# A selective-scan and expert-routing kernel: the router's sigmoid through tanh, shorter VectorE chains, the first norm's turned rows copied by VectorE, and a new order of the work in a batch

## The chip, the cores and the metric

One Trainium2 chip, one of its cores. The metric is the device time of one execution in microseconds (us), of which the median of several runs is taken. Matmuls run on TensorE (PE, with its weight loads as PEld), elementwise work on VectorE (DVE) and ScalarE (ACT), one product of the scan on GpSimd (POOL), and SyncE (SP) issues DMAs.

## The reference

The input x is 32 x 750 x 256 in f32; everything is f32. Three stages follow each other, cut here to what matters:

```python
# 1: per batch row, 3 segments of 256 tokens, every second token kept (128 each)
scores = q @ k.T / sqrt(256)                       # q = k = v = x
h = softmax(scores) @ v
# 2: a selective scan on the layernormed h
x_in, z = split(layernorm(h) @ W_in.T)             # 512 + 512
u = silu(causal_conv4(x_in) + b_conv)
dt = softplus(u @ W_dt.T + b_dt);  Bm, Cm = u @ W_B.T, u @ W_C.T      # 16 states
s_n[t] = exp(dt * A_n) * s_n[t-1] + dt * u * Bm_n;  y = sum_n s_n * Cm_n
h = h + (y * silu(z)) @ W_out.T
# 3: a mixture of 64 experts on the layernormed h
score = sigmoid(layernorm(h) @ gate_w.T);  biased = score + gate_bias
# 8 groups of 8: a group's score is the sum of its two best; 4 groups stay; then the best 8 experts
weight = 2.5 * score[chosen] / sum(score[chosen])
h = h + sum over chosen of weight * expert(layernorm(h))   # at most 256 tokens per expert
```

## The kernel before, in words

The program has three phases. `sequence_phase` does stages 1 and 2 and the routing of stage 3, batch row by batch row (32 of them, called batches here, 384 tokens each). `count_phase` and `expert_phase` do the rest and are not touched.

In `sequence_phase` every engine has a `body` of 16 **steps**, k = 0 to 15, one for each state of the scan. In a step of batch b, ScalarE scales dt\*u by B (`scaled_dbu`, L374, three instructions) and takes the exponentials (`decays`, L386, four) for step k+2; TensorE turns the scaled rows into PSUM `psB` in two pieces (`turn_dbu`, L926, 4 and 8 transposes); VectorE scans in two pieces (`scan_piece`, L615, 512 and 1024 wide); GpSimd multiplies by C (L356); and TensorE sums over the states three steps later (`sum_y`, L938). `psB` has one copy: the first piece of step k+1 is turned only once the first piece of step k has been scanned, the second only after the second.

Around these steps each engine carries work of other batches, at places written out by hand in the four `body` functions: the attention of batch a = b+2, the projections, convolution and dt of n = b+1, the gate and output of m = b-1, the second norm of o = b-2, and the routing of c = b-3 (before, the router's logits themselves belong to o). Each engine runs its list in order and waits by semaphore. Small products pass through two PSUM buffers, `psM`: `SLOTTED` lists by name which product uses which buffer in which order (XN: turned rows of the first norm; X: input projection; Z: gate; D: dt; CB, BT: B and C; DU: dt\*u; YT, O: gated y and output; QT, S, PT, AT: attention; X2T: turned rows of the second norm; LG: router logits), and `LAG` which batch it belongs to. A product waits until the one before it in its buffer has been copied out. The steady batches run in a hardware loop of two batches per pass; six batches before and five after are written out.

What the change and the steps of the prediction touch:

- ScalarE's `copy_turned` (L396) copies XN, QT and X2T out of PSUM. XN0 and XN1 are copied in step 0.
- `biased_dt` (L422, L423) and `softplus` (L430, L432): an Identity and an Abs per chunk, then an Exp and a Ln per half.
- `exp_logits` (L481) is the exponential for the router's sigmoid, in step 15; on VectorE `score_experts` (L736, L738) adds one and takes the reciprocal. `score_groups` (L756 to L769) finds the two best of each group by maxima and minima, in nine instructions.
- `silu_z` (L411), `silu_u` (L416) in steps 3 and 4, with the activation table loaded before (at L411) and after (L542).
- VectorE's `row_max` (L632, L635), `newton` (L651 to L658, four instructions on three columns, twice per batch), `conv` (L712, three taps for two pairs of chunks), `gate` (L627), `norm` (L667), `add_block` (L694).
- TensorE's `turn_normed1`, `turn_normed2`, `turn_x` (all L947), `project_xin` (L995), `project_z` (L1003), `project_dt` (L1013), `project_out` (L1052), `route` (L1062).

## Time and profile before

| | |
|---|---|
| three runs | 3473.83, 3476.50, 3476.91 us; median 3476.5 |
| profiled execution | 3474.01 us; span of its instructions 3472.2 us |
| mean granted TensorE clock | 0.955 of full speed; 1.00 from 100 to 2300 us |
| busy, share of the span | PE 86%, PEld 69%, DVE 83%, ACT 82%, POOL 61% |
| HBM traffic | 68 GB/s over the span |

Busy time is the time in which an engine executes an instruction; starts and ends of one instruction overlap with its neighbours' a little. The batches run until about 2980 us, the experts from there on. A wait is put down to the instruction that released it; "issue" is idle time for which the profile shows no releaser.

### The profile page before, as it was taken

The numbers are of one execution on the slowest core, as the hardware profiler recorded it, in microseconds if no ns is written. First come the engines' busy times: TensorE is split into PE (matmuls) and PEld (weight loads), VectorE is DVE, ScalarE is ACT, GpSimd is POOL, SyncE is SP. The second block draws the span as 40 slices with busy tenths as digits, with TensorE's granted clock in tenths as the row PEclk, the third lists the DMA queues.
The fourth block names the chain that finished last, engine by engine and source line by source line (L and its number), as shares of the span: only waits on it lengthen the run. The fifth ranks groups of instructions, "written<-read, shape, count | busy, mean of one in ns | idle before, by whom it ended". The sixth has DMA issues, their size and how long they took to land. (4 is left out here: it accounts for less than half of the span.)

```text
span 3472.2 us, 62460 instructions
## 1 busy us (share of the span) xinstructions
PE 2993.6 (86%) x19009; PEld 2407.9 (69%) x19009; DVE 2874.4 (83%) x4756; ACT 2853.9 (82%) x5580; POOL 2104.8 (61%) x780
## 2 busy tenths in 40 slices
PE   6899999999999999999999999999999997576664
PEld 4777777777777777777777777777777776455543
DVE  3888999999989999999999999999999998444432
ACT  5999999999999999999999999999999995211110
POOL 0666665666656565656565666666666665177776
PEclk8999999999999999999999999999999998578887
DMA  2111222111212121112221211111211110267774
GB/s 92 51 51 60 62 62 63 50 57 62 62 63 62 54 62 48 54 61 62 63 62 63 62 59 57 63 62 63 62 63 62 58 53 27 89 142 150 149 150 81
DMA packets 187542, 241.44 MB, mean 70 GB/s; under 512 B 45152, under 2 KB 165440, under 8 KB 187200
## 3 DMA queue, kind: packets, MB, share of 16 engines
q1 hardware_dynamic: 162624, 199.44, 18.5%
q0 software_dynamic: 24576, 37.77, 6.5%
q8 instruction: 174, 2.85, 0.3%
q14 instruction: 168, 1.38, 0.1%
HBM read 176.07 MB, written 61.08 MB: 68 GB/s over the span
## 5 line engine op out<-in xcount | busy, mean ns | idle before, releaser
L356 POOL TENSOR_TENSOR hid<-hid,c_all 128x1536 f32<-128x1536 f32 x512 | 1770.2, 3457 | 1160.9 <-DVEq L610 1159.4
L615 DVE TENSOR_TENSOR_SCAN hid<-decay,hid,psB 128x1024 f32<-128x1024 f32 x512 | 1201.6, 2347 | 101.8 <-PE psB L926 60.4
L386 ACT ACTIVATE decay<-dt,a_neg 128x383 f32<-128x383 f32 x2048 | 1086.7, 607 | 0.0
L374 ACT ACTIVATE dbu_t<-dtu_t,b_t 128x512 f32<-128x512 f32 x1536 | 994.6, 715 | 41.6 <-PE psB L926 38.1
L926 PE MATMUL psB<-ident,dbu_t 128*128 128x128 f32 x6144 | 856.9, 276 | 109.8 <-DVE hid L615 103.8
L926 PEld LDWEIGHTS psB<-ident,dbu_t 128*128 128x128 f32 x6144 | 701.5, 141 | 234.6 <-DVE hid L615 133.3
L938 PE MATMUL psY<-ident,hid 128*128 128x128 f32 x6144 | 765.3, 275 | 4.0 <-DVE yz_t L627 3.6
L938 PEld LDWEIGHTS psY<-ident,hid 128*128 128x128 f32 x6144 | 695.3, 142 | 6.9 <-issue 3.8
L615 DVE TENSOR_TENSOR_SCAN hid<-decay,psB 128x512 f32<-128x512 f32 x512 | 623.8, 1218 | 72.4 <-PE psB L926 29.7
L1013 PE MATMUL psM<-u,w_dt 128*128 128x384 f32 x1024 | 355.0, 490 | 21.2 <-ACT turned L396 16.8
L1013 PEld LDWEIGHTS psM<-u,w_dt 128*128 128x128 f32 x1024 | 184.4, 190 | 131.4 <-ACT turned L396 23.7
L1427 ACT ACTIVATE e_side<-e_psL,e_in_tile 128x128 f32<-128x128 f32 x128 | 45.7, 363 | 260.0 <-DVE e_in_tile L1551 174.1
L1400 POOL DMA_INDIRECT out_dram<-e_ys,e_dst_st x128 | 205.1, 1602 | 72.5 <-issue 62.1
L712 DVE SCALAR_TENSOR_TENSOR u<-xin,w_cv,u 128x384 f32<-128x384 f32 x384 | 210.8, 611 | 12.5 <-ACT xin L404 12.3
L1003 PE MATMUL psM<-w_in,turned 128*128 128x512 f32 x384 | 178.4, 601 | 36.3 <-ACT zs_t L411 36.3
L995 PE MATMUL psM<-turned,w_in 128*128 128x384 f32 x512 | 182.2, 497 | 4.8 <-ACT xin L404 2.5
L1052 PE MATMUL psM<-w_out,yz 128*128 128x256 f32 x768 | 179.0, 383 | 0.8 <-ACT yz L468 0.8
L1513 DVE COPY e_xt<-e_psG 128x512 f32<-128x512 f32 x64 | 44.2, 691 | 156.4 <-PE e_psG L1453 137.9
L1453 PE MATMUL e_psG<-e_ident,e_xg 128*128 128x128 f32 x256 | 50.6, 330 | 131.6 <-DMA e_xg<-x_weights_dram,e_src_st 131.6
L1391 POOL DMA_INDIRECT e_xg<-x_weights_dram,e_src_st x128 | 127.5, 996 | 49.2 <-issue 37.8
L1052 PEld LDWEIGHTS psM<-w_out,yz 128*128 128x128 f32 x768 | 142.7, 193 | 18.4 <-issue 1.1
L396 ACT ACTIVATE turned<-psM 128x384 f32<-128x384 f32 x192 | 92.2, 481 | 75.2 <-PE psM L947 74.4
(149 smaller groups left out, 3348.3 us busy)
## 6 DMA issues: line engine op xcount, KB each, us to landing
c_all<-bc_rows_dram SPq DMA_DIRECT2D x128, 768.0 KB, 4.8
out_dram<-h SPq DMA_DIRECT2D x64, 384.0 KB, 5.6
h<-out_dram SPq DMA_DIRECT2D x32, 384.0 KB, 4.0
x_weights_dram<-normed SPq DMA_DIRECT2D x32, 384.0 KB, 3.3
xs<-in_x_dram SPq DMA_DIRECT2D x32, 256.0 KB
e_wg<-in_gate_dram SPq DMA_DIRECT2D x64, 128.0 KB
e_wu<-in_up_dram SPq DMA_DIRECT2D x64, 128.0 KB
e_wd<-in_down_dram SPq DMA_DIRECT2D x64, 128.0 KB
```

The costliest lines, as they stand in the source:

```text
L356: nc.gpsimd.tensor_tensor(hid[k % 4][:, :, :], hid[k % 4][:, :, :], c_all[:, k, :].unsqueeze(1).to_broadcast([P, CH, L]), ALU.mult).then_i ...
L374: last = nc.scalar.activation(dbu_t[k % 2][:, t, :], dtu_t[q][:, t, :], ACT.Copy, scale=b_t[q][:, t, k:k + 1])
L386: last = nc.scalar.activation(decay[k % 4][:, c, 1:L], dt[q][:, c, 1:L], ACT.Exp, scale=a_neg[:, c, k:k + 1])
L615: nc.vector.tensor_tensor_scan(h[:, lo:hi], flat(decay[k % 4])[:, lo:hi], flat(psB)[:, lo:hi], h[:, lo - 1:lo] if j else 0.0, ALU.mult, AL ...
L712: last = nc.vector.scalar_tensor_tensor(out=u[:, c, :], in0=xin[:, c, t:t + L], scalar=w_cv[:, c, t:t + 1], in1=u[:, c, :], op0=ALU.mult, ...
L926: last = nc.tensor.transpose(flat(psB)[:, i * P:(i + 1) * P], dbu_t[k % 2][:, t, c * P:(c + 1) * P], ident[:, :])
L938: last = nc.tensor.matmul(psY[:, t, c * P:(c + 1) * P], hid[k % 4][:, c, t * P:(t + 1) * P], ident[:, :], is_transpose=True, start=(k == 0 ...
L995: last = nc.tensor.matmul(psM[slot(name)][:, 0:L], w_in[:, k, c * P:(c + 1) * P], turned[:, k, :], start=(k == 0), stop=(k == KD - 1))
L1003: last = nc.tensor.matmul(psM[slot(name)][:, :], turned[:, k, t * P:(t + 1) * P], w_in[:, k, DI:2 * DI], start=(k == 0), stop=(k == KD - 1))
L1013: last = nc.tensor.matmul(psM[slot(name)][:, 0:L], w_dt[:, k, c * P:(c + 1) * P], u[:, k, :], start=(k == 0), stop=(k == CH - 1))
L1052: last = nc.tensor.matmul(psM[slot(name)][:, i * D:(i + 1) * D], yz[:, c, s * P:(s + 1) * P], w_out[:, c, :], start=(c == 0), stop=(c == C ...
L1400: nc.gpsimd.indirect_dma_start(out=h_out, out_offset=bass.IndirectOffsetOnAxis(ap=dst_st[q][:, h:h + 1], axis=0), in_=ys[q % 4][:, h, :], ...
```

## The change

The router's sigmoid is computed as 0.5 + 0.5 tanh(x/2): ScalarE takes the tanh in step 4, just before the third silu of the gate, one batch later than the exponential was taken (LG's lag goes from -2 to -3), and VectorE needs one instruction instead of two. TensorE's `route` moves from step 15 to step 4. The two best of a group are found in seven instructions. A Newton step has three instructions instead of four. The row maximum is taken negated in one instruction, its scale being put into the turned q (= k), D^-0.25 in QT0 and QT1. Abs of softplus reads SBUF, once per half, instead of PSUM once per chunk. XN0 and XN1 are turned at the end of the batch before (step 15) and copied out of PSUM by VectorE in step 0. Most side work gets new places in the 16 steps, and `SLOTTED` follows them. `DIAG` is empty, so the branches on it add nothing.

```diff
-ROUTE_STEPS = 15
+ROUTE_STEPS = 14
...
-SLOTTED = (("XN0", "X0", "X2", "Z0", "Z2", "D0", "D1", "D2", "X2T0", "D3", "AT0", "BT", "YT0", "DU1", "DU2",
-            "LG"),
-           ("O1", "XN1", "X1", "X3", "Z1", "QT0", "QT1", "S", "PT", "CB", "X2T1", "AT1", "YT1", "DU0", "YT2",
-            "O0"))
...
+SLOTTED = (("X0", "X2", "Z0", "Z2", "D0", "D1", "D2", "X2T0", "D3", "CB", "AT0", "YT0", "DU1", "O0", "XN1"),
+           ("O1", "X1", "X3", "Z1", "LG", "QT0", "QT1", "S", "PT", "X2T1", "BT", "AT1", "YT1", "DU0", "YT2",
+            "DU2", "XN0"))
+LAG = {**dict.fromkeys(("QT0", "QT1", "S", "PT", "AT0", "AT1", "XN0", "XN1",), 2),
+       **dict.fromkeys(("X0", "X1", "X2", "X3", "Z0", "Z1", "Z2", "D0", "D1", "D2", "D3", "CB", "BT", "DU0", "DU1", "DU2",), 1),
...
+       **dict.fromkeys(("O1", "X2T0", "X2T1",), -2),
+       **dict.fromkeys(("LG",), -3)}
...
+                by = D ** -0.25 if name in ("QT0", "QT1") else 1.0
+                nc.scalar.activation(to[:, kd, :], psM[slot(name)][:, 0:L], ACT.Copy,
+                                     scale=by).then_inc(s_out[slot(name)], 1)
...
-                nc.scalar.activation(xin[:, c, TAPS - 1:], src, ACT.Identity, bias=b_dt[:, c:c + 1])
-                nc.scalar.activation(soft[:, c, :], src, ACT.Abs, bias=b_dt[:, c:c + 1]).then_inc(s_out[slot(name)], 1)
+                nc.scalar.activation(xin[:, c, TAPS - 1:], src, ACT.Identity,
+                                     bias=b_dt[:, c:c + 1]).then_inc(s_out[slot(name)], 1)
...
+                nc.scalar.activation(soft[:, a:z, :], xin[:, a:z, TAPS - 1:], ACT.Abs).then_inc(s_de[half], 1)
+                act.wait_ge(s_de[half], 2 * n + 1)
...
+                                                bias=nmax[:, s:s + 1],
...
                 nc.scalar.activation(denom[:, :, :], psM[slot("LG")][:, 0:NSEG * NE].rearrange(
-                    "p (s e) -> p s e", s=NSEG), ACT.Exp, scale=-1.0).then_inc(s_out[slot("LG")], 1)
+                    "p (s e) -> p s e", s=NSEG), ACT.Tanh, scale=0.5).then_inc(s_out[slot("LG")], 1)
...
                     if k == 0:
                         if front:
-                            copy_turned("XN0", n, 0)
-                            copy_turned("XN1", n, 1)
+                            copy_xin(n, 0)
...
                     if k == 4:
+                        if routed:
+                            tanh_logits(c)
                         if front:
                             silu_z(n, r, 2)
                             silu_u(n)
                             act.preload_act_table_set("natural_log_exp_and_others")
-                        if early:
-                            copy_turned("QT0", a, 0)
...
+                        if early:
+                            probs(a)
...
                     if k == 9:
+                        if late:
+                            copy_turned("X2T1", o, 1)
...
-                    if k == 15:
-                        if late:
-                            exp_logits(o)
...
+            def copy_turned(name, b, kd):
+                filled(name, b)
+                to = turned2 if name in ("X2T0", "X2T1") else turned
+                nc.vector.tensor_copy(to[:, kd, :], psM[slot(name)][:, 0:L]).then_inc(s_out[slot(name)], 1)
...
-                nc.vector.tensor_reduce(rmax[:, :], psM[slot("S")][:, 0:L].rearrange("p (s k) -> p s k", s=NSEG),
-                                        AX.X, ALU.max).then_inc(s_rm, 1)
-                dve.wait_ge(s_rm, a + 1)
-                nc.vector.tensor_scalar(nmax[:, :], rmax[:, :], -(D ** -0.5), None, ALU.mult).then_inc(s_nm, 1)
+                nc.vector.tensor_reduce(nmax[:, :], psM[slot("S")][:, 0:L].rearrange("p (s k) -> p s k", s=NSEG),
+                                        AX.X, ALU.max, negate=True).then_inc(s_nm, 1)
...
-                dve.wait_ge(s_nw[j], 3 * n + 1)
-                nc.vector.tensor_tensor(t[:, 1, :], t[:, 0, :], y, ALU.mult).then_inc(s_nw[j], 1)
-                dve.wait_ge(s_nw[j], 3 * n + 2)
-                nc.vector.tensor_scalar(t[:, 2, :], t[:, 1, :], -0.5, 1.5, ALU.mult, ALU.add).then_inc(s_nw[j], 1)
-                dve.wait_ge(s_nw[j], 3 * n + 3)
-                nc.vector.tensor_tensor(rstd[j][:, :], t[:, 2, :], y, ALU.mult).then_inc(s_rs[j], 1)
+                dve.wait_ge(s_nw[j], 2 * n + 1)
+                nc.vector.scalar_tensor_tensor(out=t[:, 1, :], in0=t[:, 0, :], scalar=-0.5, in1=y,
+                                               op0=ALU.mult, op1=ALU.mult).then_inc(s_nw[j], 1)
+                dve.wait_ge(s_nw[j], 2 * n + 2)
+                nc.vector.scalar_tensor_tensor(out=rstd[j][:, :], in0=t[:, 1, :], scalar=1.5, in1=y,
+                                               op0=ALU.add, op1=ALU.mult).then_inc(s_rs[j], 1)
...
-                nc.vector.tensor_scalar(flat(denom), flat(denom), 1.0, None, ALU.add).then_inc(s_rt, 1)
+                after(dve, s_wgt, m)
+                nc.vector.tensor_scalar(flat(score), flat(denom), 0.5, 0.5, ALU.mult, ALU.add).then_inc(s_rt, 1)
+
+            def pair_experts(m):
+
                 routed_to(m, 1)
-                nc.vector.reciprocal(flat(score), flat(denom)).then_inc(s_rt, 1)
-
-            def pair_experts(m):
-
-                routed_to(m, 2)
                 nc.vector.tensor_tensor(biased[:, :, :], score[:, :, :],
                                         bias[:, :].unsqueeze(1).to_broadcast([P, NSEG, NE]), ALU.add).then_inc(s_rt, 1)
+                routed_to(m, 2)
+                grp = biased[:, :, :].rearrange("p t (g h k) -> p (t g) h k", g=G, h=2)
+                nc.vector.tensor_tensor(halves[:, 0, :, :], grp[:, :, 0, :], grp[:, :, 1, :], ALU.max)
+                nc.vector.tensor_tensor(halves[:, 1, :, :], grp[:, :, 0, :], grp[:, :, 1, :], ALU.min).then_inc(s_rt, 1)
+
+            def score_groups(m):
+
                 routed_to(m, 3)
-                grp = biased[:, :, :].rearrange("p t (g h k) -> p (t g) h k", g=G, h=2)
-                hi, lo = halves[:, 0, :, :], halves[:, 1, :, :]
-                nc.vector.tensor_tensor(hi, grp[:, :, 0, :], grp[:, :, 1, :], ALU.max)
-                nc.vector.tensor_tensor(lo, grp[:, :, 0, :], grp[:, :, 1, :], ALU.min).then_inc(s_rt, 1)
-
-            def score_groups(m):
-
-                hi, lo = halves[:, 0, :, :], halves[:, 1, :, :]
-                hi2, mn, mx, lo2 = (quarters[:, j, :, :] for j in range(4))
+                nc.vector.tensor_tensor(quarters[:, 0:2, :, :], halves[:, :, :, 0:2], halves[:, :, :, 2:4], ALU.max)
+                nc.vector.tensor_tensor(quarters[:, 2, :, :], halves[:, 0, :, 0:2], halves[:, 0, :, 2:4],
+                                        ALU.min).then_inc(s_rt, 1)
                 routed_to(m, 4)
-                nc.vector.tensor_tensor(hi2, hi[:, :, 0:2], hi[:, :, 2:4], ALU.max)
-                nc.vector.tensor_tensor(mn, hi[:, :, 0:2], hi[:, :, 2:4], ALU.min)
-                nc.vector.tensor_tensor(mx, lo[:, :, 0:2], lo[:, :, 2:4], ALU.max).then_inc(s_rt, 1)
+                nc.vector.tensor_tensor(quarters[:, 1, :, :], quarters[:, 1, :, :], quarters[:, 2, :, :],
+                                        ALU.max).then_inc(s_rt, 1)
                 routed_to(m, 5)
-                nc.vector.tensor_tensor(lo2, mn, mx, ALU.max).then_inc(s_rt, 1)
-                v = [best[:, j, :] for j in range(4)]
-                nc.vector.tensor_tensor(v[0], hi2[:, :, 0], hi2[:, :, 1], ALU.max)
-                nc.vector.tensor_tensor(v[1], hi2[:, :, 0], hi2[:, :, 1], ALU.min)
+                nc.vector.tensor_tensor(best[:, 0:2, :], quarters[:, 0:2, :, 0], quarters[:, 0:2, :, 1], ALU.max)
+                nc.vector.tensor_tensor(best[:, 2, :], quarters[:, 0, :, 0], quarters[:, 0, :, 1],
+                                        ALU.min).then_inc(s_rt, 1)
                 routed_to(m, 6)
-                nc.vector.tensor_tensor(v[2], lo2[:, :, 0], lo2[:, :, 1], ALU.max).then_inc(s_rt, 1)
+                nc.vector.tensor_tensor(best[:, 1, :], best[:, 1, :], best[:, 2, :], ALU.max).then_inc(s_rt, 1)
                 routed_to(m, 7)
-                nc.vector.tensor_tensor(v[3], v[1], v[2], ALU.max).then_inc(s_rt, 1)
+                nc.vector.tensor_tensor(flat(gsum), best[:, 0, :], best[:, 1, :], ALU.add).then_inc(s_rt, 1)
+
+            def pick_groups(m):
...
+                    if k == 0:
+                        if front:
+                            copy_turned("XN0", n, 0)
+                            copy_turned("XN1", n, 1)
                     if k == 1:
                         if late:
                             add_block(o, 1)
                             second_stats(o)
-                    if k == 3:
+                    if k == 2:
                         if back:
                             gate(m, r)
+                    if k == 4:
                         if front:
                             conv(n, 0, 1)
+                            conv(n, 1, 1)
+                            conv(n, 0, 2)
+                            conv(n, 1, 2)
+                            conv(n, 1, 3)
+                            conv(n, 0, 3)
+                    if k == 5:
                         if late:
                             newton(o, 1)
-                        if front:
-                            conv(n, 0, 2)
-                            conv(n, 1, 1)
-                    if k == 4:
-                        if front:
-                            conv(n, 1, 2)
-                            conv(n, 0, 3)
-                            conv(n, 1, 3)
+                            norm(o, 1, h2, normed2)
                     if k == 6:
                         if routed:
                             score_experts(c)
-                        if late:
-                            norm(o, 1, h2, normed2)
+                    if k == 7:
                         if routed:
                             pair_experts(c)
-                    if k == 7:
-                        if routed:
                             score_groups(c)
+                            pick_groups(c)
+                            pick_experts(c)
                     if k == 8:
-                        if routed:
-                            pick_groups(c)
                         if early:
                             row_max(a)
+                        if routed:
+                            choose(c)
                     if k == 9:
-                        if routed:
-                            pick_experts(c)
                         if front:
                             finish_dt(n, r, 0)
                         if routed:
-                            choose(c)
+                            weigh(c)
                     if k == 10:
                         if front:
+                            drive(n, r, 0)
                             finish_dt(n, r, 1)
-                        if routed:
-                            weigh(c)
-                        if front:
-                            drive(n, r, 0)
+                            drive(n, r, 1)
                     if k == 11:
                         if early:
                             attended(a)
-                        if front:
-                            drive(n, r, 1)
                     if k == 12:
                         if early:
                             first_stats(a)
-                    if k == 14:
+                    if k == 15:
                         if early:
                             newton(a, 0)
-                    if k == 15:
-                        if early:
                             norm(a, 0, h1, normed1)
                         if back:
                             add_block(m, 0)
@@ -915,16 +920,22 @@
...
                     if k == 0:
-                        if front:
-                            turn_normed1(n, 0)
                         if late:
                             project_out(o, 1)
                         if front:
-                            turn_normed1(n, 1)
+                            project_xin(n, 0)
                     if k == 1:
                         if front:
-                            project_xin(n, 0)
+                            project_xin(n, 1)
                     if k == 2:
                         if front:
-                            project_xin(n, 1)
                             project_xin(n, 2)
                             project_xin(n, 3)
...
                             project_z(n, 2)
+                        if routed:
+                            route(c)
+                    if k == 5:
                         if early:
                             turn_x(a, 0)
-                    if k == 5:
                         if front:
                             project_dt(n, 0)
                     if k == 6:
@@ -1113,11 +1123,11 @@
                     if k == 7:
                         if front:
                             project_dt(n, 2)
+                        if late:
+                            turn_normed2(o, 0)
                         if early:
                             scores(a)
                     if k == 8:
-                        if late:
-                            turn_normed2(o, 0)
                         if front:
...
-                    if k == 10:
                         if late:
                             turn_normed2(o, 1)
+                    if k == 10:
+                        if front:
+                            turn_b(n)
                         if early:
                             attend(a, 0)
...
-                            turn_dtu(n, 1)
                     if k == 13:
-                        if front:
-                            turn_dtu(n, 2)
                         if back:
                             turn_yz(m, 2)
+                        if front:
+                            turn_dtu(n, 1)
                     if k == 14:
+                        if front:
+                            turn_dtu(n, 2)
                         if back:
                             project_out(m, 0)
                     if k == 15:
-                        if late:
-                            route(o)
+                        if early:
+                            turn_normed1(a, 0)
+                            turn_normed1(a, 1)
```

## Rows read from the trace of the kernel before

**Rows 1.** Windows: start:end, length, then busy us and (instructions) per engine, clock, DMA.

```profile
700.00:2300.00 1600.00, 1469.94 (x9772) 1184.85 (x9771) 1483.09 (x2242) 1532.87 (x2902) 973.70 (x283) 1.00 0.19 60
...
2985.00:3472.20 487.20, 308.52 (x1270) 242.20 (x1269) 186.43 (x709) 76.98 (x329) 333.46 (x260) 0.78 0.65 130
```

**Rows 2.** Waits from 700 to 2300 us: us in total, times, longest.

```profile
DVE hid L615 <- PE psB L926: 40.8, 76, 2.4
...
ACT turned L396 <- PE psM L947: 32.8, 35, 1.0
...
ACT dbu_t L374 <- PE psB L926: 23.1, 9, 3.5
...
DVE hid L615 <- ACT decay L386: 6.9, 12, 1.8
...
ACT yz L468 <- PE psM L947: 5.4, 17, 0.4
```

**Rows 3.** Groups by line from 700 to 2300 us: busy and mean ns, then idle before.

```profile
L411 ACT ACT_TABLE_LOAD x18 | 23.1, 1283 | 0.3
```

**Rows 4.** Timeline of ScalarE, steps 0 to 4 of one batch: start, us.

```profile
1414.73 0.47 ACT L396 ACTIVATE turned<-psM 128x384 f32<-128x384 f32 x1
1416.02 0.49 ACT L396 ACTIVATE turned<-psM 128x384 f32<-128x384 f32 x1 [0.82 <-PE psM L947]
1416.40 2.12 ACT L386 ACTIVATE decay<-dt,a_neg 128x383 f32<-128x383 f32 x4
...
1434.49 1.28 ACT L411 ACT_TABLE_LOAD   x1
1435.79 1.09 ACT L411 ACTIVATE zs_t<-psM 128x512 f32<-128x512 f32 x2
...
1438.60 0.60 ACT L411 ACTIVATE zs_t<-psM 128x512 f32<-128x512 f32 x1
1439.07 1.49 ACT L416 ACTIVATE u<-u 128x1536 f32<-128x1536 f32 x1
...
1595.34 0.47 ACT L396 ACTIVATE turned<-psM 128x384 f32<-128x384 f32 x1
```

**Rows 5.** Timeline of VectorE: what becomes of the logits, and the scaled row maximum.

```profile
1444.37 0.23 DVE L736 TENSOR_SCALAR denom<-denom 128x192 f32<-128x192 f32 x1
...
1445.90 0.96 DVE L667 TENSOR_SCALAR normed<-h,mv,rstd 128x256 f32<-128x256 f32 x3
...
1458.21 0.17 DVE L635 TENSOR_SCALAR nmax<-rmax 128x3 f32<-128x3 f32 x1
```

**Rows 6.** Groups of VectorE reading PSUM, by shape.

```profile
L1513 DVE COPY e_xt<-e_psG 128x512 f32<-128x512 f32 x64 | 44.2, 691 | 156.4 <-PE e_psG L1453 137.9 <-issue 18.4
...
L694 DVE TENSOR_TENSOR h<-psM,h 128x256 f32<-128x256 f32 x32 | 12.8, 400 | 4.3 <-PE psM L1052 4.3
```

**Rows 7.** Timeline of ScalarE, softplus.

```profile
1456.53 0.58 ACT L423 ACTIVATE soft<-psM,b_dt 128x384 f32<-128x384 f32 x1
1456.99 0.86 ACT L430 ACTIVATE soft<-soft 128x768 f32<-128x768 f32 x1
1457.88 0.85 ACT L432 ACTIVATE soft<-soft 128x768 f32<-128x768 f32 x1
```

**Rows 8.** Timeline of all engines around the loop's back edge.

```profile
1501.26 0.65 PE L926 MATMUL psB<-ident,dbu_t 128*128 128x128 f32 x4 [2.35 <-issue]
...
1502.11 1.22 DVE L615 TENSOR_TENSOR_SCAN hid<-decay,psB 128x512 f32<-128x512 f32 x1 [1.99 <-PE psB L926]
...
1504.13 2.35 DVE L615 TENSOR_TENSOR_SCAN hid<-decay,hid,psB 128x1024 f32<-128x1024 f32 x1 [0.81 <-PE psB L926]
```

**Rows 9.** Timelines of TensorE (routing logits, third gate product) and VectorE (last taps).

```profile
1408.60 1.45 PE L1062 MATMUL psM<-w_gt,turned 128*128 128x64 f32 x12
...
1436.44 1.98 PE L1003 MATMUL psM<-w_in,turned 128*128 128x512 f32 x4 [1.18 <-ACT zs_t L411]
...
1434.02 3.24 DVE L712 SCALAR_TENSOR_TENSOR u<-xin,w_cv,u 128x384 f32<-128x384 f32 x6
```

102 lines of the change are left out of this document (50 added, 52 removed).

## The prediction

> **What bounds the kernel now.** First the windows: the batches fill the time to about 2980 us, and the experts take the last 487.2 us at their own pace, with GpSimd and DMA the busiest; nothing in them is edited [rows 1]. So what the change is worth is read from the steady batches. The same copy of XN0 stands at 1414.73 and, two batches on, at 1595.34 us: 180.6 us for a pass of the loop, **90.3 us per batch** [rows 4]. The 1600 us from 700 to 2300 hold 283 instructions of GpSimd, one per step, or 283 / 16 = 17.7 batches [rows 1]. Divided by that, TensorE is busy 83.0 us per batch, VectorE 83.8, ScalarE 86.6 [rows 1]: three engines near the limit, and no single one that bounds.
>
> Then the waits [rows 2]. VectorE's scans wait 40.8 us for turned rows and 6.9 for decays, 2.7 us per batch; the rest of its idle time is gaps between its own dependent instructions. So 90.3 - 2.7 = 87.6 us of a batch are VectorE's own. ScalarE waits 32.8 + 23.1 + 5.4 us, 3.5 per batch; 86.8 are its own. A change that takes work from only one of the two gains little; this one takes from both.
>
> One wait has a cause apart from the work. At the loop's back edge TensorE stands still for 2.35 us before the first transposes of step 0, with no releaser, and VectorE then loses 1.99 + 0.81 = 2.8 us [rows 8], once in two batches, so 1.4 of its 2.7 us per batch. ScalarE's wait for the same transposes is the 23.1 us in 9 times of [rows 2].
>
> **The change part by part, per batch.** VectorE first.
> - Logits: from the add (1444.37) to the norm behind the reciprocal (1445.90) are 1.53 us; one scalar instruction of 0.23 us stays [rows 5]: -1.3.
> - Two instructions fewer in finding the two best of a group, one fewer in each of two Newton steps, one fewer in the row maximum. The removed ones are small, like the scaled row maximum's 0.17 us [rows 5]. The last three give -0.5; the first two -0.2, since one of the remaining is wider (between 0 and -0.34).
> - The copies of XN0 and XN1 come to it. No row shows 384 columns from PSUM to SBUF alone; 256 wide an add takes 0.40 us and 512 wide a copy 0.69 [rows 6]. Halfway is 0.55, so +1.1 for both, between 0.8 and 1.4.
>
> Sum -0.9 (-1.3 to -0.5). But the copies stand in step 0, ahead of the scan that waits at the back edge. In every second batch they fall into that 2.8 us wait, if the turned rows are there: TensorE now turns them before the back edge. That hides half of their cost: -0.55 more.
>
> ScalarE: from the first copy (1414.73) to the decays behind the second (1416.40) are 1.67 us, of which 0.82 is a wait for TensorE [rows 4]; so -0.85 of work and a wait gone. Abs: one of 384 columns from PSUM takes 0.46 us from its start to the next, four of them 1.8; the Exp of 768 columns takes 0.89 to the start of the Ln that depends on it, and two Abs of that form cost 1.8 [rows 7]. So -0.05 and no more: the gain is only that TensorE gets the D slots back 0.46 us earlier. The tanh costs what the exponential did, and the scale in the q copies is an immediate: 0. Sum -0.9: 85.9 us its own.
>
> For such a copy the Trainium skill speaks against moving it ("VectorE: DVE Perf Modes", the TRN2 errata): it gives 120 + N cycles from PSUM on VectorE and 172 + N on ScalarE. At its clocks (0.96 and 1.2 GHz) that is an estimated 0.53 and 0.46 us for 384 columns; this trace agrees on ScalarE with 0.47 [rows 4]. By it the two copies would cost 1.05 us where the sum has 1.1, so dearer than on the engine they leave, which only matters where VectorE bounds.
>
> TensorE: the same matmuls; 83.0 us stay, and it is the engine with room.
>
> **The moved work.** Step 4 gets worse for ScalarE. Before, the third gate product started at 1436.44 behind a wait of 1.18 us for the first silu and took 1.98 [rows 9]; the third silu began at 1438.60 [rows 4], just in time. Now TensorE adds the routing logits, 1.45 us [rows 9], and ScalarE wants them **ahead** of the third silu. That is a new wait of some 1.3 us; behind it queue the silu of u, the table load, the decays of step 6 and TensorE's first dt product. Against it go the 0.82 us of XN1, and the rest of the 32.8 us that copies of turned rows wait (32.8 / 17.7 - 0.8 = 1.0), mostly X2T0, which is now turned a step earlier. So ScalarE's waits go from 3.5 to 3.5 - 0.8 - 1.0 + 1.3 = 3.0, and its chain to 85.9 + 3.0 = 88.9.
>
> The convolution becomes one block of six passes in step 4; three passes took 3.24 us [rows 9], so 6.4 together. No work is added, and the gate moves from step 3 to 2, where it may wait for the last `sum_y`; and in step 15 the first output product comes one dt\*u turn later and scan piece 1 with it. I put these at +0.15 on VectorE, nothing at best and 1.0 at worst. VectorE: 90.3 - 0.9 - 0.55 + 0.15 = 89.0, which meets ScalarE's 88.9. The router's SP stores, the C loads and GpSimd move by less than a step and are covered by GpSimd's 39% of idle time (973.70 busy of 1600 [rows 1]); without that cover each step would cost GpSimd's own 3.5 us, still under VectorE's.
>
> **Forecast:** 90.3 - 89.0 = 1.3 us per batch, 32 batches, 42 us. Before the first and behind the last scan the chains get some tenths shorter and a table load for the tanh may come: nothing. The profiled execution took 3474.0 us, 0.07% under the median of 3476.5. 3474 - 42 = **3432 us**, with its own range from 0.7 to 1.9 us per batch: 3413 to 3452.
>
> **Rivals.**
> - **More waits go than work.** The new places even out TensorE's list: of the four input projections one falls in step 0, one in step 1 and two in step 2, where there were none, one and three. If VectorE's 1.3 us of waits away from the back edge go too and step 4 costs nothing, 1.45 + 1.05 = 2.5 us per batch: 3394. ScalarE allows it (85.9 plus half of the back edge is about 87). For: both engines lose work. Against: the step 4 wait. 23%.
> - **Given back.** The new waits of steps 2, 4 and 15 take 1.0 us more than assumed: within 0.2% of before, about 3474. 10%.
> - **Slower: ScalarE held twice at step 4.** First by the routing logits, then by the silu of u, which needs the end of the convolution block. Before, ScalarE had 1.9 us in hand there: the last passes began at 1434.02 and took 3.24, the silu began at 1439.07 [rows 4, 9]. Its other waits after the change are 1.7 us, so it is even with before at 90.3 - 85.9 - 1.7 = 2.7 us in step 4, and decides from there. If scans 2 and 3 run late and the block ends 2.4 us behind ScalarE's arrival, on top of 1.3, that is 3.7: 1.0 us per batch slower, 3474 + 32 = 3506. For: six passes in a row with nothing for TensorE to turn. Against: the passes' inputs are ready long before, and the gate and Newton no longer stand between them. 11%.
> - **The tanh is not in the silu's table.** Then each batch has a load before and after it, 1.28 us each [rows 4], 2.6 on ScalarE: 85.9 + 2.6 + 2.7 of waits = 91.2, +0.9 per batch, 3503. No row of this trace shows a tanh; against it: one load serves the three silus of a batch and the Copies that ScalarE scales rows with between them (18 loads in 17.7 batches [rows 3]), so the silu's table holds more than the silu. 3%. 
>
> **Chances.** Forecast 53%, 3394 23%, equal 10%, slower 11% + 3%. A measurement here tells about 0.2% (7 us) from no change. Faster by more than that 0.76, within it 0.10, slower 0.14. The range, 3388 to 3472, holds the forecast and most of the better case, and leaves out the equal and slower ones.
>
> **What the profile after would show.** Right: a spacing of batches near 89.0 us; the reciprocal gone; VectorE's new copies about 0.55 us each, without wait behind the back edge; ScalarE's wait on turned rows below 1 us per batch, and one of about 1 us at the tanh for the logits; two table loads per batch as before; VectorE's wait at the back edge around 1.5 us. Wrong: a wait at the tanh or silu of u over 2.7 us; more than two loads; copies at 0.7 us or more; gate or scan pieces of steps 2, 3 and 15 that wait over 1 us; or a spacing under 88.4, by which waits would have gone and not only work.

## The result, and the profile after

The changed kernel takes 3447.8 us (median of 4 runs, 3442.8 to 3450.8): a ratio of 0.9917 to before, 95% interval 0.9900 to 0.9934. A second measurement, among the experiments, gives 0.9936 [0.9922, 0.9949]; one of its six runs took 7641 us; it is left out of the ratio, and nothing on record explains it. Forecast were 3432 us with a range of 3388 to 3472. The direction and the range are right, the gain is smaller: 29 us, or by the second measurement 22, where 42 were forecast. In this document 1% of 3472 us over 32 batches is 1.085 us per batch, so the gain is **0.7 to 0.9 us per batch** instead of 1.3. The experiments ran on two chips, each beside the kernel before on the same chip; where a run is compared with after across them, both of after's ratios are taken as bounds.

The window over the steady batches answers to [rows 1], with 286 steps of GpSimd, 17.9 batches, where 283 stood:

```profile
700.00:2300.00 1600.00, 1476.54 (x9901) 1193.73 (x9900) 1493.68 (x2182) 1532.84 (x2860) 988.80 (x286) 1.00 0.19 60
```

Divided by 17.9, VectorE is busy 83.5 us per batch (before 83.8): the work that was taken from it hardly shows. ScalarE's fell from 86.6 to 85.7.

ScalarE's timeline gives the period by the copy of X0, two batches apart, and step 4 (start, duration, idle time before in brackets):

```profile
1408.75 0.67 ACT L415 ACTIVATE u<-psM,b_cv,w_cv 128x384 f32<-128x384 f32 x1 [0.34 <-PE psM L1006]
...
1431.94 0.33 ACT L496 ACTIVATE denom<-psM 128x192 f32<-128x192 f32 x1 [1.04 <-PE psM L1073]
1432.17 0.59 ACT L424 ACTIVATE zs_t<-psM 128x512 f32<-128x512 f32 x1
1432.64 1.49 ACT L429 ACTIVATE u<-u 128x1536 f32<-128x1536 f32 x1
...
1587.87 0.67 ACT L415 ACTIVATE u<-psM,b_cv,w_cv 128x384 f32<-128x384 f32 x1 [0.34 <-PE psM L1006]
```

179.12 us for two batches, 89.56 per batch, where [rows 4] had 90.3. Both are passes in which TensorE ran at full clock throughout. That was not so in all: taken from one silu of u to that two batches on, ten passes from about 630 to 2430 us, TensorE's granted clock fell for a stretch to the lower of its two levels (1.2 instead of 2.4 GHz) in 4 of 10 passes of before, in 1 of after and in 4 of the second measurement of after. The passes without such a stretch took 180.3, 179.1 and 179.1 us on average, those with it 1.4 to 2.2 more. At full clock the change is thus worth 0.6 us per batch. The 1.00 that the table of before has from 100 to 2300 us is a rounded mean over these stretches.

The tanh waits 1.04 us for the logits; the silu of u behind it waits for nothing.

The waits from 700 to 2300 us (total, times, longest), against [rows 2]:

```profile
ACT dtu_t L476 <- PE psM L958: 22.0, 18, 1.2
...
ACT denom L496 <- PE psM L1073: 18.7, 18, 1.0
DVE hid L626 <- PE psB L937: 16.1, 28, 0.8
...
PE psM L958 <- ACT xin L435: 12.9, 18, 0.8
ACT u L415 <- PE psM L1006: 12.4, 17, 1.1
...
ACT dbu_t L385 <- PE psB L937: 9.6, 18, 1.2
...
DVE turned L635 <- issue: 7.0, 9, 1.0
...
DVE yz_t L643 <- ACT xin L417: 5.4, 9, 0.8
```

VectorE's waits for others fell from 2.7 us per batch to (16.1 + 5.4) / 17.9 = 1.2. So waits went, 1.5 us, and VectorE's own list, 89.56 - 1.2 = 88.4 (0.4 of it the idle time without a releaser at the back edge), did not get shorter than the 87.6 of before. ScalarE waits 62.7 / 17.9 = 3.5 us as before, at new places; its own work is 89.56 - 3.5 = 86.1 (before 86.8). One wait is to be remembered, that of TensorE's turning (L958) for the copy `xin` (L435): 0.7 us in each batch, for which the trace of before shows no wait.

The groups by line show VectorE's copies and the table loads ahead of the first silu; behind the silu of u there are as many, 18 (busy, mean ns, idle before):

```profile
L424 ACT ACT_TABLE_LOAD x18 | 23.1, 1283 | 0.3
...
L635 DVE COPY turned<-psM 128x384 f32<-128x384 f32 x35 | 17.7, 547 | 7.0 <-issue 7.0
```

Around the back edge, TensorE's and VectorE's timeline, where [rows 8] had 2.35, 1.99 and 0.81:

```profile
1491.00 2.35 DVE L626 TENSOR_TENSOR_SCAN hid<-decay,hid,psB 128x1024 f32<-128x1024 f32 x1 [0.79 <-PE psB L937]
1493.42 0.65 PE L937 MATMUL psB<-ident,dbu_t 128*128 128x128 f32 x4 [1.80 <-DVE hid L626]
1494.19 1.02 DVE L635 COPY turned<-psM 128x384 f32<-128x384 f32 x2 [0.84 <-issue]
```

VectorE loses 0.84 us there and 0.79 in the scan ahead of it, not 2.8. Over the nine back edges from 700 to 2300 us the first of the two is 0.66 to 1.00 us. Before, the two waits together took 2.1 to 2.8 us at full clock, so that the 2.8 of [rows 8] is the largest, and 3.8 to 3.9 where the clock had fallen.

Where did VectorE's removed work go? Its timeline in steps 6 and 7:

```profile
1439.08 0.23 DVE L751 TENSOR_SCALAR score<-denom 128x192 f32<-128x192 f32 x1
1439.23 1.22 DVE L626 TENSOR_TENSOR_SCAN hid<-decay,psB 128x512 f32<-128x512 f32 x1
...
1442.90 0.33 DVE L756 TENSOR_TENSOR biased<-score,bias 128x192 f32<-128x192 f32 x1
...
1445.28 0.31 DVE L786 MAX8 gtop<-gsum 128x8 f32<-128x8 f32 x3 [0.15 <-DVE gsum L779]
...
1447.62 1.22 DVE L626 TENSOR_TENSOR_SCAN hid<-decay,psB 128x512 f32<-128x512 f32 x1
```

The logits cost 0.15 us of the list instead of 1.53. But the choice of experts, from `biased` to the scan behind it, takes 4.72 us in one block. The same instructions, two more among them, filled 4.32 us before, spread over four steps, 6 to 9 (4.60 as the mean of 18 batches; in every second one an idle time of 0.36 us without a releaser stood among them). Packed together, each waits for the one before it, and a gap that a neighbour used to fill is open.

VectorE's whole list can be added up over 18 batches, each instruction counted from its start to the next one's start, with waits for other engines and the idle time at the back edge taken out. It is 87.5 us per batch against 87.4. The logits gave 1.4, the Newton steps and the row maximum 0.8. Against that stand the copies with 0.9, weights and dt with 0.3, the choice with 0.1, the convolution with 0.1, the norms and other small places with 0.4, and the scans, with what is lost between two of them, with 0.4.

### The profile page after: what moved, and what is told of

Its sections match the earlier page's. It is cut to its first block and busy times, and to the rows that moved or that the text cites. A ratio compares the mean times of both kernels' runs of the same rounds, so it can differ in the third digit from the quotient of the medians.

```text
span 3449.1 us, 62714 instructions
## 1 busy us (share of the span) xinstructions
PE 2980.5 (86%) x19009; PEld 2395.9 (69%) x19009; DVE 2866.7 (83%) x4628; ACT 2833.6 (82%) x5457; POOL 2105.2 (61%) x780
## 5 line engine op out<-in xcount | busy, mean ns | idle before, releaser
L937 PEld LDWEIGHTS psB<-ident,dbu_t 128*128 128x128 f32 x6144 | 697.9, 141 | 290.0 <-DVE hid L626 183.0
L1014 PE MATMUL psM<-w_in,turned 128*128 128x512 f32 x384 | 180.3, 606 | 41.1 <-ACT zs_t L424 40.1
L1063 PE MATMUL psM<-w_out,yz 128*128 128x256 f32 x768 | 179.1, 384 | 0.7 <-issue 0.7
L1014 PEld LDWEIGHTS psM<-w_in,turned 128*128 128x128 f32 x384 | 68.4, 191 | 111.7 <-issue 61.5
```

What stands on the lines that cost most here:

```text
L937: last = nc.tensor.transpose(flat(psB)[:, i * P:(i + 1) * P], dbu_t[k % 2][:, t, c * P:(c + 1) * P], ident[:, :])
L1014: last = nc.tensor.matmul(psM[slot(name)][:, :], turned[:, k, t * P:(t + 1) * P], w_in[:, k, DI:2 * DI], start=(k == 0), stop=(k == KD - 1))
L1063: last = nc.tensor.matmul(psM[slot(name)][:, i * D:(i + 1) * D], yz[:, c, s * P:(s + 1) * P], w_out[:, c, :], start=(c == 0), stop=(c == C ...
```

## The experiments

Two theories stood at the start. One: VectorE's list sets the pace, and its instructions add up. The rival, which grew out of the first runs: the three engines are tied together step by step through `psB` and the two buffers of `psM`, and an edit is worth what it does to one such tie.

**One reciprocal back.** The kernel after, with a reciprocal whose output nothing uses:

```diff
+                nc.vector.reciprocal(flat(spare), flat(denom))
```

> The changed kernel with one reciprocal of 128x192 more per batch on VectorE, its result unused. VectorE bounds the changed kernel (theory A): the 1.35 us it takes lengthen every batch, spacing 89.6 to 90.9 us, 3447 + 43 = about 3488 us, ratio to before 1.002 to 1.005. ScalarE bounds it (theory B): it lies in VectorE's waits, spacing stays near 89.6, ratio 0.991 to 0.994.

Measured: 3472.98 us, ratio 1.0004 [0.9995, 1.0013]. It gives back the whole gain, 0.7 to 0.9 us per batch for an instruction of 1.35. In the passes at full clock it is 1.1. In the order of after, VectorE's time mostly counts.

**The small arithmetic alone, in the order of before:**

```diff
-                nc.scalar.activation(xin[:, c, TAPS - 1:], src, ACT.Identity, bias=b_dt[:, c:c + 1])
-                nc.scalar.activation(soft[:, c, :], src, ACT.Abs, bias=b_dt[:, c:c + 1]).then_inc(s_out[slot(name)], 1)
+                nc.scalar.activation(xin[:, c, TAPS - 1:], src, ACT.Identity,
+                                     bias=b_dt[:, c:c + 1]).then_inc(s_out[slot(name)], 1)
...
+                nc.scalar.activation(soft[:, a:z, :], xin[:, a:z, TAPS - 1:], ACT.Abs).then_inc(s_de[half], 1)
...
```

and with it, as in the change, the short Newton step, the negated row maximum and the seven maxima.

> The kernel before with the shorter Newton step, the negated row maximum with its scale in the turned q, the two best of a group in seven instructions, and Abs once per half from SBUF; order of work, slots, the router's exponential and reciprocal, and the copies of XN as before. Theory A (VectorE's own 87.6 us and its waits add up): -0.6 us of VectorE's work per batch, spacing 89.7, 19 us less, ratio 0.994 to 0.996. Theory B (ScalarE bounds and these are VectorE's alone): nothing, ratio 0.999 to 1.001.

Measured: 3467.56 us, 0.9991 [0.9983, 1.0000]: 0.1 us per batch, where the forecast had 0.7 on VectorE for these edits, and 0.05 on ScalarE. VectorE's waits for turned rows rose from the 40.8 us of [rows 2]:

```profile
DVE hid L619 <- PE psB L926: 63.3, 112, 2.5
```

**The reciprocal alone taken from before**, so that the scores are 1 + exp(-x) and the routing is another:

```diff
-                nc.vector.tensor_scalar(flat(denom), flat(denom), 1.0, None, ALU.add).then_inc(s_rt, 1)
+                nc.vector.tensor_scalar(flat(score), flat(denom), 1.0, None, ALU.add).then_inc(s_rt, 1)
...
-                nc.vector.reciprocal(flat(score), flat(denom)).then_inc(s_rt, 1)
+                dve.sem_inc(s_rt, 1)
```

> The kernel before without the reciprocal of the router's sigmoid: the scores are 1 + exp(-x), and the routing follows them; the work of the experts stays the same in shape. 1.35 us less of VectorE in step 6, nothing moved. Theory A: 1.0 to 1.35 us per batch less, ratio 0.987 to 0.991. Theory E: in step 6 TensorE's dt products are what scan 7 waits for next, so it is mostly turned into a wait: ratio 0.995 to 0.999.

Measured: 3465.33 us, 0.9986 [0.9977, 0.9995]: 0.15 us of 1.35.

```profile
DVE hid L615 <- PE psB L927: 61.2, 95, 2.5
```

The two runs say the same: in the old order, little of VectorE's time counts. 1.35 us less work becomes mostly more waiting for TensorE's turned rows (61.2 us where 40.8 stood). A part of this waiting is TensorE's clock: behind the standstill at the back edge it fell in 4 of 10 passes of before, in 7 with the small arithmetic and in 6 without the reciprocal, for instance in before (a window as in [rows 1], the clock third from the end):

```profile
1319.00:1322.00 3.00, 3.00 (x14) 3.00 (x15) 1.22 (x1) 1.24 (x3) 1.63 (x1) 0.50 0.05 11
```

The passes without such a stretch took 180.3, 179.5 and 179.8 us. So at full clock the small arithmetic is worth 0.4 us per batch and the reciprocal 0.2, and the clock took some of that back. These counts come from one profiled execution of each kernel.

**The order alone**: after, with the arithmetic of before (the diff of the second run undone, on the kernel after).

> The changed kernel with its order, slots, tanh and XN copies, but the Newton step, the row maximum and its scale, the maxima of a group and Abs as before the change. Theory E (the order and the reciprocal's end carry the gain, the small chains little, as e2_arithmetic_only showed with 0.1%): ratio 0.992 to 0.995, at most 0.3% over the changed kernel. Theory A (in the new order VectorE's work counts in full): 0.6 to 0.8 us per batch more, ratio 0.997 to 0.999.

Measured: 3504.39 us, 1.0091 [1.0075, 1.0106]. The new order with tanh and moved copies, but the old small arithmetic, is **slower than before** by 1.0 us per batch, and 1.7 to 1.9 above after. The waits point to one place:

```profile
PE psM L961 <- ACT soft L437: 32.4, 17, 1.9
DVE rmax L647 <- PE psM L987: 29.6, 17, 2.6
ACT normed L462 <- DVE nmax L650: 22.5, 17, 2.1
```

TensorE's transposes of X2T0 wait 1.9 us for the buffer that holds D2 until ScalarE has taken Identity and Abs from it; the attention scores queue behind them, and the row maximum and the probabilities wait for those. Two kernels on one chip, with after beside them, divided this in two.

**Only Abs as before**, on the kernel after (the second run's diff above, its lines undone):

> The kernel after with one thing of before: Abs of the softplus reads PSUM again, once per chunk of 384 columns (0.46 us each), and so TensorE gets the D slot back about 0.46 us later. Run e6 (all the old small arithmetic in the new order) cost 1.9 us per batch, and its trace shows TensorE's transposes X2T0 waiting 1.9 us for the slot of D2. If the slot is what costs (theory: ScalarE's slot release in steps 6 and 7), this run gives most of it back: 1.0 to 1.9 us per batch, a ratio of 1.000 to 1.009 to before, and the wait of X2T0 for D2 is 1.5 us or more. If my prediction's price for Abs (0.05 us, no more) holds, the ratio stays at 0.991 to 0.993. Between them, 0.995 to 0.999 would say that it carries a part.

Measured: 3495.14 us, 1.0072 [1.0059, 1.0085].

**Only VectorE's small chains as before**, for instance

```diff
-                nc.vector.tensor_reduce(nmax[:, :], psM[slot("S")][:, 0:L].rearrange("p (s k) -> p s k", s=NSEG),
-                                        AX.X, ALU.max, negate=True).then_inc(s_nm, 1)
+                nc.vector.tensor_reduce(rmax[:, :], psM[slot("S")][:, 0:L].rearrange("p (s k) -> p s k", s=NSEG),
+                                        AX.X, ALU.max).then_inc(s_rm, 1)
+                dve.wait_ge(s_rm, a + 1)
+                nc.vector.tensor_scalar(nmax[:, :], rmax[:, :], -(D ** -0.5), None, ALU.mult).then_inc(s_nm, 1)
```

> The kernel after with the old small chains of VectorE (four-instruction Newton steps, row maximum in two instructions, nine-instruction maxima) and the new Abs. If VectorE bounds by its own list and the prediction's price holds, these five instructions cost their 0.7 us per batch: a ratio of 0.998 to 1.000. If the slot released by Abs is what e6 showed, this run is close to after, 0.992 to 0.996. If they act through waits (the row maximum and the probabilities behind it, the selection block), more than their own time: 1.001 to 1.006. The costs of this run and of the one with the old Abs need not add up to e6's 1.9 us; if their sum is well below or above it, the edits are coupled.

Measured: 3455.09 us, 0.9954 [0.9942, 0.9966].

**The kernel after unchanged, on the same chip:**

> The kernel after, unchanged, on the same chip as the three runs beside it, so that they are compared with it and not with another day's run: 0.990 to 0.9935 by every theory.

Measured: 3448.51 us, 0.9936 [0.9922, 0.9949].

So Abs is worth 1.0072 - 0.9936 = 1.36%, **1.5 us per batch**; VectorE's five small instructions about 0.2 us, an amount whose intervals overlap (in the passes at full clock it is 0.2 too). Together 1.7, which is all of the difference to the order alone. The place can be read in the run with the old Abs (ScalarE, TensorE, VectorE):

```profile
1470.74 0.58 ACT L435 ACTIVATE xin<-psM,b_dt 128x384 f32<-128x384 f32 x1
1471.20 0.58 ACT L436 ACTIVATE soft<-psM,b_dt 128x384 f32<-128x384 f32 x1
...
1471.84 0.55 PE L956 MATMUL psM<-ident,normed 128*128 128x128 f32 x3 [1.91 <-ACT soft L436]
1472.23 2.04 PE L982 MATMUL psM<-turned 128*128 128x128 f32 x12
...
1474.31 0.56 DVE L646 TENSOR_REDUCE nmax<-psM 128x3 f32<-128x384 f32 x1 [1.89 <-PE psM L982]
...
1474.90 0.37 ACT L461 ACTIVATE normed<-psM,nmax 128x128 f32<-128x128 f32 x1 [1.12 <-DVE nmax L646]
```

and in after, the same instructions:

```profile
1448.75 0.58 ACT L435 ACTIVATE xin<-psM,b_dt 128x384 f32<-128x384 f32 x1
...
1449.38 0.55 PE L958 MATMUL psM<-ident,normed 128*128 128x128 f32 x3 [0.67 <-ACT xin L435]
1449.77 1.50 PE L984 MATMUL psM<-turned 128*128 128x128 f32 x12
...
1451.31 0.56 DVE L648 TENSOR_REDUCE nmax<-psM 128x3 f32<-128x384 f32 x1
```

The tanh of the same batch stands at 1453.05 in the one and 1431.94 in the other, 21.11 us apart; the X2T0 transposes are 22.46 apart. The transposes come 1.35 us later, about three times 0.46: three Abs (D0, D1, D2) stand in ScalarE's list ahead of D2's release, not one. The batch shown is one of those in which TensorE's clock fell behind the wait, so that its scores, and the waits for them, are longer than in the others. But the passes at full clock say the same. They took 179.1 us on average in after and 181.7 with the old Abs:

```profile
1182.21 1.49 ACT L429 ACTIVATE u<-u 128x1536 f32<-128x1536 f32 x1
...
1363.93 1.49 ACT L429 ACTIVATE u<-u 128x1536 f32<-128x1536 f32 x1
```

That is 1.3 us per batch from the wait alone. In before the scores came **ahead** of the X2T0 transposes, and those 2.1 us behind D2's release (its Abs in [rows 7], then the next at 1456.99):

```profile
1455.15 1.50 PE L973 MATMUL psM<-turned 128*128 128x128 f32 x12
...
1459.11 0.49 PE L947 MATMUL psM<-ident,normed 128*128 128x128 f32 x3
```

So there TensorE does not wait for D2's release, and the small arithmetic in the old order, with the same new Abs, gained 0.1 us in all (0.4 at full clock).

**The choice of experts spread** over steps 6 to 10 again, with the mask of the chosen in step 9 and the weights in step 10, on the kernel after:

```diff
-                    if k == 7:
                         if routed:
                             pair_experts(c)
+                    if k == 7:
+                        if routed:
                             score_groups(c)
-                            pick_groups(c)
-                            pick_experts(c)
                     if k == 8:
+                        if routed:
+                            pick_groups(c)
...
                     if k == 9:
+                        if routed:
+                            pick_experts(c)
...
```

> The changed kernel with the router's selection spread over steps 6 to 10 again, as before the change, scans between its parts, in place of one block in step 7. Same instructions. Theory C: in a block every instruction waits for the result of the one before (0.15 us of exposed latency at each joint), which cost 0.4 us per batch against the kernel before where 0.2 were to be saved; spread, VectorE's own work falls by 0.4 to 0.7 us per batch, 13 to 22 us, ratio 0.985 to 0.988. Rival D: the place does not matter to VectorE's own time, or other waits appear: ratio 0.991 to 0.993.

Measured: 3476.14 us, 1.0012 [1.0003, 1.0021]. A miss: VectorE's own time did fall by some 0.7 us (the choice itself from 4.72 to 4.48), as the open joints had suggested, but the kernel became 0.8 to 1.0 us per batch slower.

```profile
DVE hid L626 <- PE psB L941: 37.7, 49, 2.1
ACT dbu_t L385 <- PE psB L941: 35.7, 43, 3.0
...
DVE nmax L648 <- PE psM L988: 15.4, 18, 1.1
```

The block of step 7 stands where TensorE has a long step (a dt product, X2T0 and the scores); it fills a time in which VectorE would wait. This reading is argued from the waits: they grew, but no run moved TensorE's step 7.

**Joints opened elsewhere**: the second norm to step 6, the pairs with it, and the weights between the two dt parts of step 10.

```diff
-                            norm(o, 1, h2, normed2)
                     if k == 6:
...
+                        if late:
+                            norm(o, 1, h2, normed2)
...
                             finish_dt(n, r, 1)
+                        if routed:
+                            weigh(c)
```

> The changed kernel with three joints opened and the block of step 7 otherwise kept: the biased scores and first halves go to step 6, the second norm from step 5 to 6, and the weights from step 9 to between the dt parts of step 10. Same instructions. Theory C (exposed latency between dependent instructions is VectorE's own time): 0.3 to 0.5 us per batch less, ratio 0.986 to 0.989. Theory E (what VectorE does in steps 5, 7 and 9 covers TensorE's dt products there, and leaving it uncovers them): waits take it back or more, ratio 0.992 to 0.999.

Measured: 3459.99 us, 0.9962 [0.9948, 0.9976]: 0.3 to 0.5 us per batch worse than after. VectorE's waits for TensorE are 28.2 us in it and TensorE's for VectorE 76.1, each above after's 16.1 and 67.3.

**The routing logits ahead of the third gate product** on TensorE:

```diff
-                        if front:
-                            project_z(n, 2)
                         if routed:
                             route(c)
+                        if front:
+                            project_z(n, 2)
```

> The changed kernel with TensorE's routing logits ahead of the third gate product in step 4, so that they fill the 1.15 us in which TensorE waits for the first silu. The wait of 1.04 us before the tanh goes. Theory A (VectorE bounds): ScalarE has only more slack, ratio 0.990 to 0.993 as the changed kernel. Theory B (ScalarE bounds): up to 1.0 us per batch less, ratio 0.982 to 0.985.

Measured: 3465.08 us, 0.9984 [0.9975, 0.9994], 0.5 to 0.7 us per batch above after. A miss of its premise: the logits' buffer is the one of Z1, so `route` itself waits for the second silu, and the third silu comes later still.

```profile
ACT zs_t L424 <- PE psM L1014: 34.2, 18, 3.1
...
PE psM L1073 <- ACT zs_t L424: 29.7, 18, 1.7
```

ScalarE's wait grew from 1.04 to 1.9 us, +0.86, and 0.5 to 0.7 of it reached the period: ScalarE's time in step 4 counts too. A part of it came through TensorE's clock, which fell in 8 of the 10 passes, behind the wait of 1.7 us for the second silu; the two others took 179.7 and 180.1 us, 0.4 per batch more than after's.

**The copies of XN0 and XN1 by ScalarE in step 0**, still turned in step 15:

```diff
+                            copy_turned("XN0", n, 0)
+                            copy_turned("XN1", n, 1)
                             copy_xin(n, 0)
```

> The changed kernel with XN0 and XN1 copied by ScalarE in step 0 again, ahead of X0; they are still turned in step 15. Theory A (VectorE's own work sets the spacing where it leaves no waits): VectorE loses 0.95 us of work per batch, but ScalarE gets 0.85 and its copies of X0 come later, so a half of it at best: ratio 0.987 to 0.992. Theory E (the three engines are coupled step by step, and any work added to ScalarE's chain before step 4 comes out behind the silus): 0.4 to 0.9 us per batch more, ratio 0.995 to 1.000.

Measured: 3582.75 us, 1.0332 [1.0316, 1.0348]. It doesn't price the copies, since it makes another wait: ScalarE comes to them behind its dt\*u rows, and the second output product O1 needs XN0's buffer.

```profile
ACT u L415 <- PE psM L1004: 77.8, 17, 6.1
DVE h L710 <- PE psM L1061: 60.1, 17, 4.5
...
PE psM L1061 <- ACT turned L408: 47.1, 17, 3.1
```

What it shows: turned at the end of the batch before, these rows need an engine that is free at once in step 0. What two such copies would cost on ScalarE in their old place under the new order was not tried.

**A candidate: dt\*u turned a step earlier** by TensorE.

```diff
                             turn_yz(m, 1)
-                    if k == 12:
                         if front:
                             turn_dtu(n, 0)
+                    if k == 12:
+                        if front:
+                            turn_dtu(n, 1)
...
-                            turn_dtu(n, 1)
-                    if k == 14:
-                        if front:
                             turn_dtu(n, 2)
+                    if k == 14:
```

> A candidate that could beat after: TensorE turns dt*u one step earlier (the second part in step 12, the third in step 13 behind the last turned gated y), so that steps 14 and 15 are lighter for it. Theory (the coupling sits step by step between TensorE and VectorE): the scan of the first piece of state 15 waits 0.79 us in every batch of after, and ScalarE 1.2 us for the first part of dt*u; both should fall to about half, 0.4 us per batch, a ratio of 0.987 to 0.989. Rival: the load only moves to steps 12 and 13, which then wait instead, and the ratio stays within 0.991 to 0.993, or becomes worse if VectorE's dt*u is not ready a step earlier.

Measured: 3595.68 us, 1.0353 [1.0332, 1.0374], 4.5 us per batch above after. Neither number was near. Its waits, and TensorE's timeline in step 12:

```profile
PE psM L958 <- ACT yz L483: 90.2, 49, 3.0
ACT yz L483 <- PE psM L958: 53.4, 17, 4.3
```

```profile
1452.64 0.67 PE L958 MATMUL psM<-ident,u 128*128 128x128 f32 x4 [3.00 <-ACT yz L483]
```

The parts of dt\*u and of the gated y alternate in the two buffers, and ScalarE's copies of them had stayed in their steps. TensorE, a step early, stood still three times per batch. Here a product moved ahead without the copy that frees its buffer gained nothing. No run beat the kernel after.

## Why the prediction was right, and where not

**The sign and the range** held. Of the forecast's terms, these came as written or nearly: the tanh needs no load of its own (18 loads of each kind in 17.9 batches, [rows 3] had 18 in 17.7), so that rival falls; the wait at the tanh is 1.04 us where 1.3 was put, and the silu of u waits for nothing, so "held twice at step 4" falls; ScalarE's own work is 86.1 us (85.9 forecast); a copy takes 0.547 us (0.55 forecast).
**The step that failed first: "-0.05 and no more: the gain is only that TensorE gets the D slots back 0.46 us earlier."** In the new order Abs is worth 1.5 us per batch, the largest single term of the change; in the passes at full clock it is 1.3, which is the wait alone. I priced the release of the slot by one Abs and did not follow it to the product that waits for it. The rows would have led on: three Abs stand ahead of D2's release, X2T0 is next in that buffer, and the diff itself puts X2T0's transposes ahead of the scores in step 7.

**The second: the new order at "+0.15 on VectorE".** By the forecast's terms, order, tanh and copies without the small arithmetic came to -1.3 + 1.1 - 0.55 + 0.15 = -0.6 us per batch; measured is +1.0. The waits of steps 2, 4 and 15 were looked for, and they are small. That of step 7, which the order makes and the new Abs takes away again, was missed. The two misses, +1.6 and -1.0 (the small arithmetic: 0.7 forecast, 1.7 to 1.9 in this order), partly cancel, and so the sum came near. That was luck: it was nearer than its terms.

**The third: VectorE's "Sum -0.9".** The removed instructions are gone, and gave 2.2 us where 1.8 were put, but the list did not get shorter: 88.4 us, or 88.0 without the back edge's idle time, instead of 86.7. The term took the place of an instruction to cost nothing. Against the forecast -0.2 the choice rose by 0.1; weights and dt, the convolution, the norms and the other small places rose by 0.8 together, and the scans with their seams by 0.4. That packing does this is shown for the choice, the weights and dt, by the run that spreads them; for the rest it is argued. Putting the choice apart again (the run with it spread) is no way out, since its block also covers TensorE's step 7.

**"That hides half of their cost".** VectorE's wait at the back edge, once in two batches, was to go from 2.8 to around 1.5 us. It is 0.84. But the 2.8 was the largest of its kind at full clock. The 0.79 us in the scan ahead of it is new, and comes in every batch. How much of the copies is hidden has no run of its own.

**Waits.** "More waits go than work" was given 23%. VectorE's did fall by 1.5 us per batch, and its work by nothing. As a mechanism that rival was nearer than the forecast, but its 3394 us assumed that the work would go too. **TensorE's clock** is a term that the prediction does not have: it was lower in 4 of 10 passes of before and in 1 and 4 of 10 of the two profiles of after, at 1.4 to 2.2 us per such pass.

What stays open: what the tanh and the moved copies are worth each without the new order wasn't tried, nor after with the scores ahead of X2T0 again, which would try the account of Abs from the other side. The runs show that the parts don't add: the small arithmetic alone -0.1 us per batch, the order alone +1.0, both -0.7 to -0.9.

## What to carry to other kernels

Where several engines are near their limit and share buffers, price an edit by the tie it moves: for each buffer that a product waits for, count everything in the releasing engine's list ahead of the release, and ask who queues behind the waiting product. In this kernel an instruction removed was worth its time only in an order in which its engine was late; measured alone in the old order it may show nothing, and a new order measured alone may show a loss. When a product is moved ahead, move the copy that frees its buffer with it, and expect dependent instructions packed into one block to cost more than the same ones spread out.

## What the runs showed of the hardware

A standstill of TensorE can cost twice. In the run with the old Abs, the stretch with its wait and the two behind it (windows as in [rows 1], the clock third from the end):

```profile
1468.00:1471.80 3.80, 1.94 (x6) 0.79 (x5) 3.54 (x6) 3.80 (x9) 2.97 (x1) 1.00 0.00 0
1471.80:1475.00 3.20, 3.16 (x20) 3.16 (x21) 1.31 (x5) 2.05 (x4) 0.47 (x1) 0.69 0.00 0
1475.00:1478.00 3.00, 3.00 (x22) 3.00 (x21) 2.02 (x7) 3.00 (x10) 2.04 (x1) 0.76 0.00 0
```

After 1.9 us without a matmul the granted clock averages 0.69 and 0.76 of full speed, a mix of its two levels, 2.4 and 1.2 GHz, and the scores take 2.04 us instead of 1.50. In after, behind a wait of 0.67 to 0.76, they took 1.50 in each of 18 batches. With the old Abs the wait was 1.9 us in every batch, and they took 1.88 to 2.76 in 7 of 17; in the run of the order alone, with the same wait, 1.81 to 2.77 in 11 of 17. So part of the 1.5 us is the slower clock behind the wait: the six passes with such a stretch took 183.0 to 186.3 us, the four others 181.7 to 181.8.

The clock doesn't fall behind every wait of that size, and the wait's length alone doesn't decide it. In the back edge of after shown above TensorE stands for 1.80 us, and the twelve transposes behind it take their usual 1.47. At the twelve back edges from 590 to 2590 us it stood for 1.67 to 2.35 us in before, and the clock fell at 5 of them; in after for 1.60 to 2.22, and it fell at 2; in after's second measurement for 1.70 to 2.18, and it fell at 4.

At the back edge itself, VectorE has 0.84 us of idle time with no releaser even where its input is ready (L635 above), once per pass of the loop; in the other passes it was 0.66 to 1.00.
